# Graph network stack on one Trainium2 core: merge of layer one with both branches normed together, x and rows stored in one step

## The chip, the core and the metric

The kernel runs on one core of one Trainium2 chip. The metric is the time on the device in microseconds (us), from the start to the end of one execution; lower is better. Engines: PE (TensorE), DVE (VectorE), ACT (ScalarE), POOL (GpSimd), SP (SyncE, which here only issues transfers).

## What is computed

A stack of four graph layers over 6250 nodes with 256 features and 106250 edges, each a residual on a pre-normed input. Two places matter here: how layer zero's result enters x, and the end of layer one, where an attention branch over the edges (`h_local`) and a branch from a scan over the nodes sorted by degree (`y`) are merged. Cut to that:

```python
h = maximum(layernorm(x), 0); x = x + L0(h, ...)
h = maximum(layernorm(x), 0)                      # rows, h_dram
# layer one, on h (called x inside the layer)
agg = segment_sum(proj[src] * attn, tgt)
h_local = layer_norm(elu(agg + x + gat_b), ln_local_g, ln_local_b)
y = mamba(x[perm], ...)
h_attn = layer_norm(x + y[inv], ln_global_g, ln_global_b)
gate = sigmoid(h_local @ wl.T + h_attn @ wg.T)
h = gate * h_local + (1 - gate) * h_attn
ff = relu(h @ ff1_w.T + ff1_b) @ ff2_w.T + ff2_b
x = x + layer_norm(h + ff, ln2_g, ln2_b)
h = maximum(layernorm(x), 0)                      # input of layer two
```

## The kernel before

The program is a row of stages, most of them closed by a barrier. Nodes are held in T = 49 blocks of 128 rows. Dense work on nodes runs in *lanes* (`in_lanes`, L163): seven of them, each with its own tile slices, its own PSUM bank and its own semaphore. A job is two blocks (25 jobs, the last of one block). A stage is a Python generator; every `yield` ends a turn of its lane. The program is written turn by turn: in each turn every running lane puts one step into the engines' queues, in lane order, and then `beside` puts in what runs alongside. Lane k starts at turn `stagger * k`; a lane that is done starts its next job three turns later. The engines run their queues in order.

`Chain` (L72 on) makes a lane's steps follow one another. `step` waits on the engine for all that the chain has done so far, issues its instructions and counts the last one. `apart` does the same for instructions on several engines, and counts each. `move` issues transfers from the lane's carrier; whatever step comes next waits for their landing. The carrier is SP for lanes 0, 2, 4 and 6, and POOL for lanes 1, 3 and 5. `layer_norm` (L480) is six steps: statistics (L486) and their aggregation (L489) on DVE, epsilon (L490) on DVE, the power -1/2 on POOL (L491), mean times that on DVE (L492), and scaling on ACT (L493); with gain and shift there are two more on DVE (L496, L497). `turn_blocks` (L509) is a PE step of transposes (L513) and an ACT step that copies them out of PSUM (L518). `elu` (L522) is three steps (L524 to L526).

**Closing stage**, `close_and_project` (L2030), stagger 4. Per job: load of sums, residual rows and x (L2034, L502) and two empty turns; four DVE steps; tanh on ACT (L2043); two DVE steps; elu; one addition (L2047); the store of x (L2048) and two empty turns; the norm; the store of the rows h (L2052); a scatter of h by POOL into the sorted order (L2053) and two empty turns; turning, projection (L2061), copy, scores (L2064), and stores (L2070, L2072). 34 turns.

**Merge**, `merge` (L2499), stagger 8. Beside it, `return_rows` puts one indirect gather per turn on POOL (L2485), 49 in all, which bring the scan's rows back in node order; a semaphore counts each ten of them. Weights are loaded by ACT before (L2461 to L2472) and waited for once, at L2526, in job 0. Per job: load of sums and rows (L2512) and two empty turns; the denominators (L2516 to L2519); agg times their reciprocals (L2521); two additions (L2523, L2527); then the local branch (elu, norm, turning), the wait for the returned rows, the scan branch (addition L2533, norm, turning), the gate's eight products into one bank (L2538), tanh (L2541), three DVE steps (L2542 to L2544), four times a first feed-forward product (L2546) and relu (L2548), the load of x into `ha` (L2549), the second product (L2551) with h added by identity (L2554), the bias (L2557), the norm with gain and shift, the addition to x (L2559), its store (L2560), the last norm and its store (L2562). 63 turns.

The order around the change is thus written by the turn counts alone; there is no planner.

Of the kernel before, what the change touches and what calls it, by code (L numbers as in the profile page):

```python
# [21 lines left out]
ALU = mybir.AluOpType  # L22
ACT = mybir.ActivationFunctionType
# [4 lines left out]
P = 128  # L28
N, D, E = 6250, 256, 106250
T = -(-N // P)  # L30
NP = T * P
TAIL = N - (T - 1) * P
LANES = 7
# [151 lines left out]
def graph_stack_kernel(nc, a, out):  # L185
# [4 lines left out]
    with root:  # L190
        def sem(name):
            return root.enter_context(nc.semaphore(name))
# [11 lines left out]
        sb = maker(root, "sb")  # L204
# [68 lines left out]
        eps = sb("eps", [P, 1])  # L273
        power = sb("power", [P, 2])
        chain.apart((pool, lambda: pool.iota(iota[:, :], [[1, P]], base=0, channel_multiplier=0,
# [233 lines left out]
        def turn_blocks(ch, dst4, src3, ps, gain=None, shift=None):  # L509

            for b in range(0, src3.shape[1], 2):
                m = min(2, src3.shape[1] - b)
                yield ch.step(pe, *[lambda k=k, c=c: pe.transpose(ps[:, c, k, :], src3[:, b + k, c * P:(c + 1) * P], ident[:, :])  # L513
                                    for k in range(m) for c in range(2)])
                if gain is None:
                    yield ch.step(act, lambda: act.activation(dst4[:, :, b:b + m, :], ps[:, :, 0:m, :], ACT.Copy))
                else:
                    yield ch.step(act, *[lambda c=c: act.activation(dst4[:, c, b:b + m, :], ps[:, c, 0:m, :], ACT.Identity,  # L518
                                                                    scale=gain[:, c:c + 1], bias=shift[:, c:c + 1])
                                         for c in range(2)])  # L520

        def elu(ch, x, tmp, out):  # L522

            yield ch.step(dve, lambda: dve.tensor_scalar(tmp, x, 0.0, None, ALU.min))  # L524
            yield ch.step(act, lambda: act.activation(tmp, tmp, ACT.Exp))
            yield ch.step(dve, lambda: dve.scalar_tensor_tensor(out, tmp, -1.0, x, ALU.add, ALU.max))  # L526
# [1456 lines left out]
        with ExitStack() as local:  # L1983
# [34 lines left out]
            with ExitStack() as inner:  # L2018
# [11 lines left out]
                def close_and_project(ch, k, b0, m):  # L2030
# [16 lines left out]
                    yield ch.step(dve, lambda: dve.tensor_tensor(x3, x3, part[0], ALU.add))  # L2047
                    yield ch.move(lambda e: e.dma_start(blk(x_dram), x3))  # L2048
                    yield
                    yield  # L2050
                    yield from layer_norm(ch, x3, t3, stat[:, k, :, :], relu=True)
                    yield ch.move(lambda e: e.dma_start(blk(h_dram), t3))  # L2052
                    yield ch.scatter(pool, *[lambda b=b: pool.indirect_dma_start(  # L2053
# [403 lines left out]
        vecs = {}  # L2457
# [18 lines left out]
        with ExitStack() as local:  # L2476
# [17 lines left out]
            xT, yT = (lsb(n, [P, 2, GB, P]) for n in ("hlT", "haT"))  # L2494
            stat = lsb("stat1", [P, LANES, 2, 8])
            bank = lps("bank2", [P, LANES, 512])
            chain.wait(act)

            def merge(ch, k, b0, m):  # L2499
# [6 lines left out]
                fT += [t3.rearrange("p b d -> p (b d)")[:, j * m * P:(j + 1) * m * P] for j in range(2)]  # L2506
                st, tn = stat[:, k, :, :], bank[:, k, :].rearrange("p (c q n) -> p c q n", c=2, q=2)
                o_ps = bank[:, k, :].rearrange("p (b d) -> p b d", d=D)
# [18 lines left out]
                yield ch.step(dve, lambda: dve.tensor_tensor(l3, l3, bv("gat_b"), ALU.add))  # L2527
                yield from elu(ch, l3, t3, l3)
                yield from layer_norm(ch, l3, l3, st)
                yield from turn_blocks(ch, lT, l3, tn, vecs["ln_local_g"], vecs["ln_local_b"])  # L2530

                dve.wait_ge(returned[b0 // PART_OF], 16 * min(PART_OF, T - b0 // PART_OF * PART_OF))
                yield ch.step(dve, lambda: dve.tensor_tensor(a3, h3, y_all[:, b0:b0 + m, :], ALU.add))  # L2533
                yield from layer_norm(ch, a3, a3, st)
                yield from turn_blocks(ch, aT, a3, tn, vecs["ln_global_g"], vecs["ln_global_b"])
                gT = bank[:, k, 0:2 * m * P].rearrange("p (c b n) -> p c b n", c=2, b=m)
# [8 lines left out]
                for j in range(4):  # L2545
                    yield ch.step(pe, *[lambda c=c: pe.matmul(ff, f1[:, c, j * P:(j + 1) * P], lT[:, c, :, :],  # L2546
                                                              start=(c == 0), stop=(c == 1)) for c in range(2)])
                    yield ch.step(act, lambda: act.activation(fT[j], ff, ACT.Relu, bias=fb[:, j:j + 1]))  # L2548
                yield ch.move(lambda e: e.dma_start(a3, blk(x_dram)))  # L2549
                yield ch.step(pe, *[f for b in range(m) for f in  # L2550
# [6 lines left out]
                yield ch.step(dve, lambda: dve.tensor_tensor(l3, o_ps[:, 0:m, :], bv("ff2_b"), ALU.add))  # L2557
                yield from layer_norm(ch, l3, l3, st, gain=vecs["ln2_g"][:, :], shift=vecs["ln2_b"][:, :])
                yield ch.step(dve, lambda: dve.tensor_tensor(a3, a3, l3, ALU.add))  # L2559
                yield ch.move(lambda e: e.dma_start(blk(merged_x[:, :]), a3))  # L2560
                yield from layer_norm(ch, a3, l3, st, relu=True)
                yield ch.move(lambda e: e.dma_start(blk(hidden[0][0:NP, :]), l3))  # L2562

# [45 lines left out]
```

## Time and profile before

| | us |
|---|---|
| median of 3 runs (lowest, highest) | 7790.14 (7788.18, 7800.23) |
| the profiled execution, its own time | 7791.36 |
| its span, first to last instruction | 7789.4 |
| closing stage of layer zero | about 2674 to 3042 |
| merge of layer one | about 4814 to 5346 |

The profiled execution is 1.2 us above the median. Busy time of an engine is the sum of its instructions; what an engine waited for is read from the waits, where each idle stretch is put down to the semaphore that came last. Landing is the time from a transfer's issue to its last byte's count.

### The profile page before, as it was taken

The numbers are of one execution on the slowest core, as the hardware profiler recorded it, in microseconds if no ns is written. First come the engines' busy times: TensorE is split into PE (matmuls) and PEld (weight loads), VectorE is DVE, ScalarE is ACT, GpSimd is POOL, SyncE is SP. The second block draws the span as 40 slices with busy tenths as digits, with TensorE's granted clock in tenths as the row PEclk, the third lists the DMA queues.
The fourth block names the chain that finished last, engine by engine and source line by source line (L and its number), as shares of the span: only waits on it lengthen the run. The fifth ranks groups of instructions, "written<-read, shape, count | busy, mean of one in ns | idle before, by whom it ended". The sixth has DMA issues, their size and how long they took to land. (4 is left out here: it accounts for less than half of the span.)

```text
span 7789.4 us, 93332 instructions
## 1 busy us (share of the span) xinstructions
PE 5313.0 (68%) x20089; PEld 3414.3 (44%) x20089; DVE 5065.8 (65%) x10805; ACT 3288.2 (42%) x11052; POOL 4469.2 (57%) x4306
## 2 busy tenths in 40 slices
PE   4656688888888545657777774775666665656555
PEld 4623344444444333224444442654444443444444
DVE  7677588888888753569999994664555553333333
ACT  1124466666666423778988894441000000000000
POOL 2150166666666253057777773324777775777775
PEclk9978899999999756779999996997888787888887
DMA  5114488888888663379998996223555556555556
GB/s 197 22 63 110 156 274 278 276 285 278 276 279 280 197 207 117 112 250 321 321 321 316 322 308 167 76 68 107 177 178 180 176 181 126 170 170 165 170 171 134
DMA packets 544576, 1554.19 MB, mean 200 GB/s; under 512 B 135295, under 2 KB 245899, under 8 KB 528650
## 3 DMA queue, kind: packets, MB, share of 16 engines
q0 software_dynamic: 234976, 829.97, 36.1%
q1 hardware_dynamic: 280348, 694.68, 25.2%
q10 hardware_dynamic: 28844, 25.07, 1.0%
q8 instruction: 138, 2.26, 0.1%
q14 instruction: 270, 2.21, 0.1%
HBM read 1183.69 MB, written 593.47 MB: 228 GB/s over the span
## 5 line engine op out<-in xcount | busy, mean ns | idle before, releaser
L1263 POOL DMA_INDIRECT rows_e<-hidden,unit_src x1856 | 1765.5, 951 | 628.5 <-issue 542.9
L618 POOL DMA_INDIRECT rows_e<-table,unit_src x928 | 1071.3, 1154 | 803.9 <-PE acc_e L823 385.8
L1000 POOL DMA_INDIRECT rows_e<-table,unit_src x928 | 1069.1, 1152 | 373.8 <-issue 269.0
L1291 DVE SCALAR_TENSOR_TENSOR sums_e<-sums_e,unit_keep,acc_e 128x256 f32<-128x256 f32 x928 | 444.1, 479 | 1212.1 <-PE acc_e L1372 1209.6
L1372 PE MATMUL acc_e<-rows_e,same 128*128 128x256 f32 x1856 | 707.1, 543 | 666.5 <-DMA rows_e<-hidden,unit_src 651.1
L812 ACT ACTIVATE rows_e<-rows_e 128x64 f32<-128x64 f32 x4640 | 1119.1, 333 | 1.9
L1084 ACT ACTIVATE rows_e<-rows_e 128x64 f32<-128x64 f32 x3712 | 919.9, 333 | 3.8
L1372 PEld LDWEIGHTS acc_e<-rows_e,same 128*128 128x128 f32 x1856 | 487.7, 278 | 845.9 <-DMA rows_e<-hidden,unit_src 708.5
L1416 ACT ACTIVATE turned_f<-turn_f 128x512 f32<-128x512 f32 x98 | 58.5, 597 | 1882.3 <-PE turn_f L1388 1882.3
L823 PE MATMUL acc_e<-rows_e,unit_w 128*128 128x512 f32 (+1 forms) x1856 | 704.9, 526 | 144.7 <-DVE rows_e L805 101.0
L1372 PE MATMUL acc_e<-rows_e,links 128*128 128x256 f32 x1856 | 514.3, 425 | 324.5 <-DMA rows_e<-hidden,unit_src 324.1
L823 PE MATMUL acc_e<-rows_e,hot_e 128*128 128x512 f32 (+1 forms) x1856 | 640.1, 498 | 26.7 <-ACT rows_e L812 20.1
L1372 PEld LDWEIGHTS acc_e<-rows_e,links 128*128 128x128 f32 x1856 | 366.9, 207 | 466.2 <-DMA rows_e<-hidden,unit_src 417.4
L823 PEld LDWEIGHTS acc_e<-rows_e,unit_w 128*128 128x128 f32 x1856 | 353.7, 200 | 424.4 <-issue 355.0
L805 DVE TENSOR_TENSOR rows_e<-rows_e 128x896 f32<-128x896 f32 x464 | 502.3, 1083 | 30.7 <-ACT rows_e L782 29.8
L823 PEld LDWEIGHTS acc_e<-rows_e,hot_e 128*128 128x128 f32 x1856 | 344.4, 190 | 322.2 <-issue 252.6
L847 DVE SCALAR_TENSOR_TENSOR sums_e<-sums_e,unit_keep,acc_e 128x780 f32<-128x780 f32 x406 | 413.5, 1019 | 96.3 <-PE acc_e L823 87.5
L2275 DVE TENSOR_TENSOR_SCAN hs<-decay,state,inp 128x896 f32<-128x896 f32 x224 | 464.2, 2072 | 11.7 <-ACT decay L2286 9.4
L2297 PE MATMUL y_ps<-prod_t,ident 128*128 128x448 f32 x900 | 435.1, 611 | 0.0
L491 POOL TENSOR_TENSOR stat<-stat,power 128x2 f32<-128x2 f32 (+1 forms) x150 | 124.8, 839 | 379.2 <-DVE stat L490 378.2
L1880 PE MATMUL tab_ps<-wt,hn 128*128 128x512 f32 x588 | 308.0, 659 | 1.9 <-DVE score_at L1858 1.9
L2266 DVE TENSOR_TENSOR inp<-bc,dtx_s 128x896 f32<-128x896 f32 x224 | 242.1, 1081 | 4.8 <-issue 4.8
(467 smaller groups left out, 9548.2 us busy)
## 6 DMA issues: line engine op xcount, KB each, us to landing
bc<-bc_rows SPq DMA_DIRECT2D x228, 896.0 KB, 6.6
summed<-sums_e SPq DMA_DIRECT2D x464, 390.0 KB
staged<-sums_e SPq DMA_DIRECT2D x116, 1024.0 KB, 4.5
summed<-sums_e SPq DMA_DIRECT2D x464, 130.5 KB
rows_e<-table,unit_src POOLq DMA_INDIRECT x1856, 5.6
hots<-hot_e SPq DMA_DIRECT2D x116, 256.0 KB, 5.0
hots<-unit_w SPq DMA_DIRECT2D x116, 256.0 KB, 4.9
rows_e<-hidden,unit_src POOLq DMA_INDIRECT x1856, 2.8
```

Source lines behind the costliest of these rows:

```text
L618: pool.indirect_dma_start(self.rows[:, v, e, :], None, table, bass.IndirectOffsetOnAxis(unit_src[:, u, e:e + 1], 0)).then_inc(self.landed[ ...
L805: dve.tensor_tensor(r, r, by.unsqueeze(3).broadcast_to([P, 2, n, DH]), ALU.mult).then_inc(self.s_mul, 1)
L812: last = act.activation(r, r, ACT.Copy, scale=self.rows[:, v, e, self.WIDTH + h:self.WIDTH + h + 1])
L823: mm = pe.matmul(self.acc[:, v % 2, a0:a1], self.hot_of(v)[:, e, :], self.rows[:, v, e, a0:a1], start=(e == 0), stop=(e == 1))
L847: dve.scalar_tensor_tensor(self.sums[:, at_, :], before, unit_keep[:, ds(u, 1)], self.acc[:, v % 2, 0:AW], ALU.mult, ALU.add).then_inc(sel ...
L1000: pool.indirect_dma_start(self.rows[:, v, e, :], None, self.tab, bass.IndirectOffsetOnAxis(unit_src[:, u, e:e + 1], 0)).then_inc(self.land ...
L1084: last = act.activation(r, r, ACT.Copy, scale=self.rows[:, v, e, D + h:D + h + 1])
L1263: pool.indirect_dma_start(self.rows[:, v, e, :], None, tab, bass.IndirectOffsetOnAxis(unit_src[:, u, e:e + 1], 0)).then_inc(self.landed[v ...
L1291: dve.scalar_tensor_tensor(self.sums[:, at_, :], self.sums[:, (n - 1) % self.SUMS, :], unit_keep[:, u:u + 1], self.acc[:, n % self.ACCS, 0 ...
L1372: mm = pe.matmul(self.acc[:, n % self.ACCS, 0:D], self.hot_of(n)[:, e, :], self.rows[:, v, e, :], start=(e == 0), stop=(e == 1))
L2275: dve.tensor_tensor_scan(hs[:, b, :], decay, inp[:, b, :], state[:, ds(STEPS * m + k, 1)], ALU.mult, ALU.add).then_inc(s_scan, 1)
L2297: mm = pe.matmul(y_ps[:, z, 0:HS], ident[:, :], prod[:, b, z * HS:(z + 1) * HS], start=False, stop=False, skip_group_check=True)
```

## The change

`power`, the tile of exponents, becomes four columns wide, and the statistics tile of the merge holds four blocks a lane. In the closing stage the store of x and the store of h become one step behind the norm, and the two empty turns go. In the merge the exponential of elu stands beside the addition of the scan branch; both branches, four blocks, are normed together; the wait for the returned rows comes ahead of the exponential; the scaling of the scan branch runs beside the turning of the local one. The load of x is issued by ACT, on a semaphore of its lane's own, and only the addition waits for it. The two stores at the end become one step.

```diff
-        power = sb("power", [P, 2])
+        power = sb("power", [P, 4])
...
                     yield ch.step(dve, lambda: dve.tensor_tensor(x3, x3, part[0], ALU.add))
-                    yield ch.move(lambda e: e.dma_start(blk(x_dram), x3))
-                    yield
-                    yield
                     yield from layer_norm(ch, x3, t3, stat[:, k, :, :], relu=True)
-                    yield ch.move(lambda e: e.dma_start(blk(h_dram), t3))
+                    yield ch.move(lambda e: e.dma_start(blk(x_dram), x3), lambda e: e.dma_start(blk(h_dram), t3))
...
-            stat = lsb("stat1", [P, LANES, 2, 8])
+            stat = lsb("stat1", [P, LANES, 4, 8])
...
+            x_in, drawn_x = [sem(f"x_in{k}") for k in range(LANES)], [0] * LANES
...
                 yield ch.step(dve, lambda: dve.tensor_tensor(l3, l3, bv("gat_b"), ALU.add))
-                yield from elu(ch, l3, t3, l3)
-                yield from layer_norm(ch, l3, l3, st)
-                yield from turn_blocks(ch, lT, l3, tn, vecs["ln_local_g"], vecs["ln_local_b"])
-
+                yield ch.step(dve, lambda: dve.tensor_scalar(t3, l3, 0.0, None, ALU.min))
                 dve.wait_ge(returned[b0 // PART_OF], 16 * min(PART_OF, T - b0 // PART_OF * PART_OF))
-                yield ch.step(dve, lambda: dve.tensor_tensor(a3, h3, y_all[:, b0:b0 + m, :], ALU.add))
-                yield from layer_norm(ch, a3, a3, st)
-                yield from turn_blocks(ch, aT, a3, tn, vecs["ln_global_g"], vecs["ln_global_b"])
+                yield ch.apart((act, lambda: act.activation(t3, t3, ACT.Exp)),
+                               (dve, lambda: dve.tensor_tensor(a3, h3, y_all[:, b0:b0 + m, :], ALU.add)))
+                yield ch.step(dve, lambda: dve.scalar_tensor_tensor(l3, t3, -1.0, l3, ALU.add, ALU.max))
+
+                both = stat[:, k, 0:2 * m, :]
+                blocks = [(j * m + b, v[:, b, :]) for j, v in enumerate((l3, a3)) for b in range(m)]
+                mean, var = both[:, :, 6], both[:, :, 7]
...
+                yield ch.apart(*[(dve, lambda n=n, v=v: dve.bn_stats(both[:, n, 0:6], v)) for n, v in blocks])
+                yield ch.step(dve, lambda: dve.sem_inc(dve_passed, 1),
+                              *[lambda n=n: dve.bn_aggr(both[:, n, 6:8], both[:, n, 0:6]) for n, _ in blocks])
+                yield ch.step(dve, lambda: dve.tensor_scalar(var, var, 1e-5, None, ALU.add))
+                yield ch.step(pool, lambda: pool.tensor_tensor(var, var, power[:, 0:2 * m], ALU.pow))
+                yield ch.step(dve, lambda: dve.scalar_tensor_tensor(mean, mean, -1.0, var, ALU.mult, ALU.mult))
+                yield ch.step(act, *[lambda n=n, v=v: scaled(n, v) for n, v in blocks[0:m]])
+                yield ch.apart(*turned_to(l3), *[(act, lambda n=n, v=v: scaled(n, v)) for n, v in blocks[m:2 * m]])
+                yield ch.step(act, *copied(lT, vecs["ln_local_g"], vecs["ln_local_b"]))
+                yield ch.step(pe, *[f for _, f in turned_to(a3)])
+                yield ch.step(act, *copied(aT, vecs["ln_global_g"], vecs["ln_global_b"]))
...
-                yield ch.move(lambda e: e.dma_start(a3, blk(x_dram)))
+                ch.wait(act)
+                act.dma_start(a3, blk(x_dram)).then_inc(x_in[k], 16)
+                drawn_x[k] += 16
...
+                dve.wait_ge(x_in[k], drawn_x[k])
                 yield ch.step(dve, lambda: dve.tensor_tensor(a3, a3, l3, ALU.add))
-                yield ch.move(lambda e: e.dma_start(blk(merged_x[:, :]), a3))
                 yield from layer_norm(ch, a3, l3, st, relu=True)
-                yield ch.move(lambda e: e.dma_start(blk(hidden[0][0:NP, :]), l3))
+                yield ch.move(lambda e: e.dma_start(blk(merged_x[:, :]), a3), lambda e: e.dma_start(blk(hidden[0][0:NP, :]), l3))
```

`scaled` is ACT's scaling of one block by its own mean and power, `turned_to` the transposes of one branch, and `copied` the two copies out of PSUM with gain and shift.

## Rows read from the trace of the kernel before

**Rows 1.** The page: busy time, share of the span and instructions of each engine.

```profile
PE 5313.0 (68%) x20089; PEld 3414.3 (44%) x20089; DVE 5065.8 (65%) x10805; ACT 3288.2 (42%) x11052; POOL 4469.2 (57%) x4306
```

**Rows 2.** The windows of the merge: us, busy (x instructions), granted clock, DMA, GB/s.

```profile
4880.00:5312.00 432.00, 333.12 (x1466) 264.94 (x1465) 261.06 (x882) 197.84 (x421) 118.64 (x142) 0.92 0.22 68
4814.00:4880.00 66.00, 18.77 (x63) 14.78 (x64) 25.47 (x87) 15.36 (x33) 48.74 (x51) 0.56 0.53 159
```

**Rows 3.** The waits of 4880 to 5312 us: engine, line, releaser: us, times, longest.

```profile
DVE hl L2557 <- PE bank L2554: 114.6, 23, 8.2
...
PE bank L2546 <- DVE hlT L2544: 39.2, 23, 4.4
...
PE bank L2551 <- DMA ha<-x_dram: 34.7, 19, 3.4
...
PE bank L2546 <- ACT tg L2548: 13.0, 23, 0.6
PE bank L2538 <- ACT haT L518: 9.6, 21, 1.6
DVE stat L486 <- DMA merged_x<-ha: 9.3, 12, 1.2
...
PE bank L2546 <- ACT haT L2548: 2.3, 4, 0.6
```

**Rows 4.** Line 2485: ns min/median/max, first and last start us; landings.

```profile
L2485 POOL DMA_INDIRECT y_all<-sorted_y,rank_i x49: 942/957/1433, 4814.6 to 4895.9; - x49
...
DMA to landing us min/median/max: 2.7/3.0/6.9
```

**Rows 5.** Line 2541, the gate's tanh, same columns.

```profile
L2541 ACT ACTIVATE ha<-bank x25: 383/597/598, 4866.9 to 5311.7; 128x512 f32<-128x512 f32 x24, 128x256 f32<-128x256 f32 x1
```

**Rows 6.** The merge by line and form: count, busy us, mean ns, idle before.

```profile
L491 POOL TENSOR_TENSOR stat<-stat,power 128x2 f32<-128x2 f32 x96 | 83.4, 879 | 202.7 <-DVE stat L490 202.2
...
L492 DVE SCALAR_TENSOR_TENSOR stat<-stat 128x2 f32<-128x2 f32 x96 | 15.4, 161 | 16.4 <-POOL stat L491 15.9
...
L491 POOL TENSOR_TENSOR stat<-stat,power 128x1 f32<-128x1 f32 x3 | 2.1, 706 | 15.0 <-DVE stat L490 15.0
```

**Rows 7.** Transfers: issue, count, size, median us from issue to landing.

```profile
ha<-x_dram SPq DMA_DIRECT2D x14, 256.0 KB, 2.7
merged_x<-ha SPq DMA_DIRECT2D x14, 256.0 KB, 2.1
```

**Rows 8.** Issues on ACT, lines 1435 and 2472: ns min/median/max, starts.

```profile
L1435 ACTq DMA_DIRECT2D hidden<-kept_f x49: 338/343/392, 5455.6 to 6579.8; - x49
...
L2472 ACTq DMA_DIRECT2D unit_w<-w_kept x1: 4022/4022/4022, 4824.9 to 4824.9; - x1
```

**Rows 9.** Line 2549, the load of x, same columns.

```profile
L2549 SPq DMA_DIRECT2D ha<-x_dram x14: 359/360/366, 4882.8 to 5314.8; - x14
L2549 POOL DMA_DIRECT2D ha<-x_dram x11: 590/742/803, 4899.2 to 5328.6; - x11
```

**Rows 10.** The timeline of 4813 to 4842 us: start, us, engine, line, idle before.

```profile
4827.42 0.99 POOL L2485 DMA_INDIRECT y_all<-sorted_y,rank_i  x1 [0.30 <-issue]
...
4836.77 0.69 DVE L2527 TENSOR_TENSOR hl<-hl,v_gat_b 128x512 f32<-128x512 f32 x1 [5.16 <-DMA unit_w<-w_kept]
```

**Rows 11.** The tile of statistics in the merge: ns min/median/max, starts.

```profile
L491 POOL TENSOR_TENSOR stat<-stat,power x99: 557/797/1347, 4840.8 to 5340.3; 128x2 f32<-128x2 f32 x96, 128x1 f32<-128x1 f32 x3
```

**Rows 12.** Line 2043, the tanh of the closing stage, same columns.

```profile
L2043 ACT ACTIVATE rg<-rg x25: 417/630/632, 2685.9 to 2996.0; 128x512 f32<-128x512 f32 x24, 128x256 f32<-128x256 f32 x1
```

**Rows 13.** The waits of 2690 to 3042 us, columns as in rows 3.

```profile
POOL sorted_h L2053 <- DMA h_dram<-tg: 96.3, 21, 7.8
```

**Rows 14.** Transfers of the closing stage, columns as in rows 7.

```profile
x_dram<-xg SPq DMA_DIRECT2D x14, 256.0 KB, 2.6
h_dram<-tg SPq DMA_DIRECT2D x14, 256.0 KB, 2.6
```

**Rows 15.** The window of the closing stage's middle, columns as in rows 2.

```profile
2735.00:2996.00 261.00, 118.61 (x396) 86.89 (x396) 137.59 (x332) 63.87 (x113) 148.15 (x155) 0.59 0.61 200
```

More of the change, by code:

```diff
@@ L2506, in merge @@
                 fT += [t3.rearrange("p b d -> p (b d)")[:, j * m * P:(j + 1) * m * P] for j in range(2)]
-                st, tn = stat[:, k, :, :], bank[:, k, :].rearrange("p (c q n) -> p c q n", c=2, q=2)
+                st, tn = stat[:, k, 0:2, :], bank[:, k, :].rearrange("p (c q n) -> p c q n", c=2, q=2)
                 o_ps = bank[:, k, :].rearrange("p (b d) -> p b d", d=D)
@@ new lines, in merge @@
+                mean, var = both[:, :, 6], both[:, :, 7]
+                scaled = lambda n, v: act.activation(v, v, ACT.Identity, scale=both[:, n, 7:8], bias=both[:, n, 6:7])
+                turned_to = lambda v: [(pe, lambda b=b, c=c: pe.transpose(tn[:, c, b, :], v[:, b, c * P:(c + 1) * P], ident[:, :]))
+                                       for b in range(m) for c in range(2)]
+                copied = lambda to, gain, shift: [lambda c=c: act.activation(to[:, c, :, :], tn[:, c, 0:m, :], ACT.Identity,
+                                                                             scale=gain[:, c:c + 1], bias=shift[:, c:c + 1])
+                                                  for c in range(2)]
```

## The prediction

> **What bounds the kernel now.** Read the page first: no engine is busy over 68% of the span [rows 1], because the program is a row of stages with a barrier between most of them. So a change is priced inside its own stage. Two stages are touched: the one that closes layer zero and projects for layer one (2674 to 3042 us), and the merge of layer one (4814 to 5346 us). Both are written by in_lanes: seven lanes, each working on two blocks of nodes, and one step of each lane per **turn**, put into the engines' queues in lane order. A queue runs in order, so one late step holds the steps of all other lanes behind it.
>
> For the merge I read its windows [rows 2]. In the first 66 us POOL is the busy one (48.7 us: 49 row gathers of 0.96 us, one put in per turn, the last at turn 48 [rows 4]). In the 432 us that follow PE is busy 333 us (77%), DVE 261, ACT 198, POOL 119. The waits of that window [rows 3] account for PE's idle 99 us to the microsecond: 39.2 for the DVE products that open the feed-forward, 34.7 for the load of x, 13.0 and 2.3 for the relu steps, 9.6 for the turned blocks (98.8 in all). PE is the engine that paces the stage, and it stops for four causes only.
>
> **The merge, step by step.** Counting yields: before, a job takes 63 turns and a lane starts again after 66. The local and scan parts take 20 steps (elu 3, norm 6, turning 2, addition 1, norm 6, turning 2); together they take 13. The load of x and the separate store of x have no turn of their own any more. After, 54 turns, and a new start after 57. With stagger 8 and 25 jobs the last job begins at turn 222 before and 195 after. The tanh (L2541) is step 32 before and 25 after, so it stands at turns 31 to 253 before (222 turns, 4866.9 to 5311.7 us, 2.00 us a turn [rows 5]) and at 24 to 219 after. Behind turn 48 there are 205 turns before and 171 after.
>
> *Instructions.* Per job one pow, one addition of epsilon and one mean product fall away, and the pow is of four columns. Pow is 706 ns for one column and 879 for two [rows 6]; 173 ns a column gives an estimate of 1.23 us for four, against 2 x 0.88, so POOL saves 0.5 us a job, and DVE 2 x 0.16 (the mean product's row; the addition is its like). That is 13 and 8 us over the stage on engines that do not pace it: I count nothing. PE's and ACT's arithmetic is the same.
>
> *The load of x.* On the lane's own semaphore the PE step behind it no longer waits: the landing (2.7 us, median [rows 7]) lies beside ten turns. This gives PE the 34.7 us. ACT now issues it: a like issue on ACT takes 0.34 us [rows 8], so 25 x 0.34 = 8.5 us in a queue that is busy 46% of the window; nothing while that cover holds, 8.5 if it is gone. Queued behind ACT's wait are the relus and scalings of other lanes; what ACT waits for is its own relu just before (0.47 us, ending anyway). POOL and SP lose this issue, 11 x 0.74 and 14 x 0.36 us [rows 9]. DVE's new wait for x stands ten turns behind the issue, some 20 us, and passes.
>
> *The two stores in one step.* The norm behind the x store no longer waits for its landing (9.3 us of DVE idle [rows 3]; DVE does not pace, and I count nothing). What is late next is only the lane's own next load, three idle turns later.
>
> *The wait for returned rows* comes ten steps earlier. For job 0 it is at turn 11. Its tenth gather is issued at 4827.4 and the slowest landing was 6.9 us, so 4834.3; DVE stands until 4836.8 for the weights anyway [rows 4, 10]. Nothing. Job 5, the first to use the second part, starts at turn 40, long behind its gathers.
>
> *The sum of the merge.* **Head:** gathers fix the first 48 turns; two pows of 0.88 us fewer there, 2 us. **Middle:** 34 turns fewer. PE's ledger says: 34.7 us of stall go for certain, and of the other 64 us I take the share of the turns that fall away (34 of 432/2.03 = 213, 16%), 10 us: 45. Turns alone at 2.03 us (415.8 us from the last gather to the last tanh, over 205) would say 69, but would put PE at 333/363 = 92% busy. 45 puts it at 86%, and I take that. Lower end 20: the stall goes and 15 us come back as other waits, as lanes stand closer. **Tail:** 31 turns of one short job become 29 and lose two landings, 2.7 and 2.1 us [rows 7]: 5 us, ends 3 and 7. Merge: 52 us, between 25 and 78.
>
> *A rule beside this.* Pow took from 557 to 1347 ns, median 797 [rows 11], so something besides its own work stretches it. The Trainium skill (SBUF — State Buffer, on the shared port pair) says that a VectorE operation with two SBUF inputs and a GpSimd operation that reads SBUF exclude each other for a whole instruction. Denser DVE work would then lengthen pows; this is a rival below.
>
> **The closing stage.** 34 turns a job become 31 and the restart 37 becomes 34: x is stored with h, in one step. With stagger 4, tanh L2043 spans turns 7 to 130 before (310.1 us, 2.52 us a turn [rows 12]) and 7 to 121 after, nine fewer, and the last job's tail is three shorter. But 96.3 us of the stage are POOL standing in 21 waits for h to land, before its scatter [rows 13]. Those come once a job and stay, since the scatter is still the step after the store (and the h store stands 14 turns ahead of its own lane's next loads before, 37 - 23, and after, 34 - 20; with a stagger of 4 that is the same place against the other lanes' loads). Per turn without them: (310.1 - 96.3)/123 = 1.74 us, so 12 turns give 21 us. Against it: the scatter now waits for x as well, which before had two empty turns to land in. The other store's issue is 0.36 (SP) to 0.77 us (POOL), and landings are alike, 2.6 us each from SP [rows 14]; 0.5 us x 21 = 10 us. If the second 256 KB cost their full time at the stage's 200 GB/s [rows 15], 1.3 us x 21 = 27. Net 10 us, between -6 and 28 (12 turns at 2.52 less nothing comes to 30, near that end).
>
> The Trainium skill (DMA: Bandwidth & Descriptors, issuing engines are not separate DMA queues) says transfers issued from any engine interleave on the same 16 engines. By it the pair pays the bytes in full, and the closing stage's result is the lower end.
>
> **Sum:** 52 + 10 = 62 us. The profiled execution took 7791.36 us (span 7789.4 and 2 around it), 1.2 above the median of the three runs, 7790.14; from the median, **7728 us**. About 0.2% (16 us) is what a measurement here can tell from no change.
>
> **Rivals.**
> - *Turns are what is paid* (the grid's latency, not PE's work). For: a turn costs 2.03 us while the pacing engine works 1.56 us in it (333 us over 213 turns). Against: PE would be 92% busy where it is 77%. 2 + 69 + 7 + 28 = 106 us: 7684. Chance 0.22.
> - *Queues are what is paid.* More steps per turn make heads of queues later, DVE idle for the second feed-forward product (114.6 us [rows 3]) above all; the middle gives 15 to 20, the closing stage nothing: 25 us, 7765. Chance 0.14.
> - *No net effect*: as that, and each of the 75 pows costs its longest row, 1.35 - 0.88 = 0.47 us, 35 us in all, which eats the 34.7. Only head and tail are left, 7 us: 7783. It is where the shared-port rule would lead if it held for every pow. For: the spread of the pows. Against: POOL is busy 119 of 432 us, and no wait of PE in [rows 3] is for it. Chance 0.07.
> - *Slower: ACT's issue.* ACT took 4.02 us to issue the load of kept weights [rows 8]; if the 25 loads of x cost 4.02 - 0.34 = 3.7 us more each in front of relus that PE waits for, 92 us come on top: 7790 - 62 + 92 = 7820. It decides from 62/25 = 2.5 us an issue. Against: thirteen other loads of ACT stood in front of that one (L2461 to L2470), and 49 stores in a later stage took 0.34. Chance 0.05.
> - The forecast, 0.52.
>
> **Numbers.** The range runs from the first rival, with room below it, to the second: 7680 to 7765, leaving out the last two and little else. The forecast's own is 7705 to 7750. Faster: 0.52 + 0.22 + 0.14 = 0.88; within 0.2%: 0.07; slower: 0.05.
>
> **What the profile after would show.** PE's wait for x gone; the last tanh some 451 us behind the stage's first instruction instead of 498; PE over 83% busy in the middle; 75 pows in the merge; the scatter's wait for x or h above 96 us; stages outside the two unchanged. Wrong would be: PE's idle as large as before with another name, an x issue on ACT over 1 us, or the closing stage longer by over 10 us.

## The result and the profile after

The changed kernel takes 7668.16 us (median of 4 runs, 7664.3 to 7673.61) against 7789.16 us before in the same session: a ratio of 0.9843 (95% interval 0.9826 to 0.986), 121 us or 1.6% faster. The forecast was faster, by 62 us, with a range down to 7680; the time lies 12 us below it.

Where the time went is read from the barriers between stages (the semaphore waits of SP at L244), in the one profiled execution of each kernel:

| us | before | after | |
|---|---|---|---|
| closing stage (last edge product to barrier) | 393.9 | 379.5 | -14 |
| merge (barrier to barrier) | 542.4 | 429.6 | **-113** |
| of it: to the last row gather (turn 48) | 82.1 | 85.8 | +4 |
| last gather to last tanh | 415.8 | 308.7 | -107 |
| last tanh to the barrier | 44.5 | 35.1 | -9 |
| stage behind the merge, to the end | 2433.2 | 2433.6 | 0 |

The two stages make 127 us; stages that no edit touches differ by 11 us up and down between two profiles, and nearly cancel. First the page's line, then the windows of the merge after; they answer to [rows 1, 2].

```profile
PE 5301.7 (69%) x20089; PEld 3402.6 (44%) x20089; DVE 5059.9 (66%) x10755; ACT 3288.3 (43%) x11052; POOL 4403.2 (57%) x4270
```

```profile
4799.30:4865.00 65.70, 24.36 (x105) 18.70 (x105) 28.94 (x86) 18.64 (x40) 45.55 (x46) 0.69 0.55 167
4865.00:5190.00 325.00, 289.81 (x1399) 232.34 (x1399) 248.98 (x830) 194.31 (x408) 100.20 (x112) 1.00 0.28 87
```

In the middle PE is busy 89% (290 of 325 us) where it was 77%. Its 1399 matmuls take 207 ns each, where 1466 took 227 before (333.12/1466), and the granted clock is 1.00 where it was 0.92. The waits of the middle after (engine, line, releaser: us, times, longest) answer to [rows 3]:

```profile
POOL stat L2545 <- DVE stat L2544: 161.4, 21, 11.9
...
DVE hl L2575 <- PE bank L2572: 42.0, 22, 3.6
...
PE bank L2569 <- ACT tg L2564: 18.9, 22, 2.2
PE bank L2562 <- ACT tg L2564: 12.4, 22, 0.6
...
DVE stat L492 <- POOL stat L491: 5.3, 7, 1.7
```

PE's wait for x is gone, and so is its wait for the DVE products (39.2 before); DVE's idle time in front of the bias, 114.6 before, is 42.0. Of PE's 35 us of idle time in this stretch 31 are two waits for relus, every job the same. The lines of the tanh, of the gathers, and of the load of x on ACT (ns min/median/max, first and last start us) answer to [rows 4, 5, 8]:

```profile
L2557 ACT ACTIVATE ha<-bank x25: 383/597/598, 4843.1 to 5193.8; 128x512 f32<-128x512 f32 x24, 128x256 f32<-128x256 f32 x1
```

```profile
L2482 POOL DMA_INDIRECT y_all<-sorted_y,rank_i x49: 942/953/1521, 4800.1 to 4885.1; - x49
```

```profile
L2566 ACTq DMA_DIRECT2D ha<-x_dram x25: 339/366/372, 4858.1 to 5206.9; - x25
...
DMA to landing us min/median/max: 2.0/2.8/5.0
```

From the last gather to the last tanh are 171 turns in 308.7 us, 1.81 us a turn, against 2.03 before. The issue on ACT takes 0.37 us (0.34 forecast). One job after is like the next; the first window is one job of the kernel after, the three below it are jobs of the kernel before (from tanh to tanh; us, then busy time and count of PE, PEld, DVE, ACT, POOL, then granted clock, DMA share, GB/s):

```profile
4973.90:4988.60 14.70, 13.27 (x66) 10.61 (x65) 11.71 (x39) 9.01 (x19) 4.06 (x6) 1.00 0.40 126
```

```profile
5014.50:5030.20 15.70, 13.13 (x65) 10.58 (x64) 9.16 (x33) 7.93 (x17) 3.83 (x6) 1.00 0.33 102
...
5081.00:5098.90 17.90, 14.47 (x62) 11.38 (x61) 10.12 (x33) 7.19 (x16) 4.38 (x6) 0.90 0.34 104
5098.90:5134.10 35.20, 24.49 (x100) 18.93 (x98) 22.36 (x79) 14.74 (x31) 9.72 (x12) 0.85 0.24 75
```

A job's 66 matmuls cost PE 13.3 us at the full clock; in the second row before, 62 of them cost 14.5, part at the lower level. The last row is the gap between two rounds of starts before, 18 turns, with PE busy 70%. After, the gap has nine turns, and all three gaps take 14.7 us, no more than a regular spacing. How the lower level looks is seen in PE's timeline before (start, us, line, tile, count; four products a row): right after the wait for x they take 1.70 and 1.91 us, the like four later 1.03. The two windows below it give the granted clock: 0.58 behind the wait, 1.00 four microseconds later, so most of the first stretch runs at the lower of the clock's two levels, 1.2 GHz, and the second at the upper, 2.4 GHz.

```profile
5087.26 1.70 PE L2551 MATMUL bank<-f,haT 128*128 128x256 f32 x4 [0.95 <-DMA ha<-x_dram]
5088.75 1.91 PE L2551 MATMUL bank<-f,tg 128*128 128x256 f32 x4
...
5092.08 1.03 PE L2551 MATMUL bank<-f,tg 128*128 128x256 f32 x4
```

```profile
5087.20:5090.40 3.20, 3.14 (x8) 2.55 (x9) 0.46 (x1) 1.76 (x4) 0.00 (x0) 0.58 0.10 32
5091.20:5094.00 2.80, 2.80 (x19) 2.59 (x18) 0.41 (x1) 0.00 (x0) 0.00 (x0) 1.00 0.54 144
```

### The profile page after: what moved, and what is told of

It is laid out like the page before. It is cut to its first block and busy times, and to the rows that moved or that the text cites. A ratio compares the mean times of both kernels' runs of the same rounds, so it can differ in the third digit from the quotient of the medians.

```text
span 7662.5 us, 93224 instructions
## 1 busy us (share of the span) xinstructions
PE 5301.7 (69%) x20089; PEld 3402.6 (44%) x20089; DVE 5059.9 (66%) x10755; ACT 3288.3 (43%) x11052; POOL 4403.2 (57%) x4270
## 5 line engine op out<-in xcount | busy, mean ns | idle before, releaser
L618 POOL DMA_INDIRECT rows_e<-table,unit_src x928 | 1034.1, 1114 | 848.0 <-PE acc_e L823 446.0
L1000 POOL DMA_INDIRECT rows_e<-table,unit_src x928 | 1059.6, 1142 | 375.4 <-issue 270.5
L2279 DVE TENSOR_TENSOR prod_t<-bc,hs 128x896 f32<-128x896 f32 x224 | 241.8, 1080 | 0.0
```

The source lines that it names most:

```text
L618: pool.indirect_dma_start(self.rows[:, v, e, :], None, table, bass.IndirectOffsetOnAxis(unit_src[:, u, e:e + 1], 0)).then_inc(self.landed[ ...
L1000: pool.indirect_dma_start(self.rows[:, v, e, :], None, self.tab, bass.IndirectOffsetOnAxis(unit_src[:, u, e:e + 1], 0)).then_inc(self.land ...
```

## The experiments

All are read by the length of the merge from barrier to barrier in one profile each. It repeats: three kernels with the changed merge gave 429.6, 430.4 and 431.6 us (one of them on a chip whose last stage took 2775 us instead of 2434), two with the merge of before 542.4 and 546.7. Steps of 5 to 7 us in the table are thus hardly more than the 4 us between two profiles of the same merge. No profile of the kernel before was taken on the chip of e9 to e12; that the changed merge takes 430.4 us there says that the merge can be compared across the two. The closing stage took 393.7 to 397.3 us in the ten profiles that have it as before, and 380 to 385 in the five that have it as changed, 13 us less on average. Ratios are to the kernel before on the same chip, with 95% intervals; on the chip of e9 to e12 it took 8322.76 us.

| run | merge, us | ratio |
|---|---|---|
| before | 542.4 | |
| e1 closing stage alone | 546.7 | 0.9983 (0.9973 to 0.9993) |
| e8 x on its own semaphore, turn kept | 498.7 | 0.9938 (0.9916 to 0.996) |
| e2 the same without the turn | 493.2 | 0.9934 (0.9916 to 0.9952) |
| e10 both stores at the end, turn kept | 540.4 | 1.0027 (1.0017 to 1.0037) |
| e4 the same without the turn | 516.2 | 0.9978 (0.9968 to 0.9989) |
| e11 normed together, 7 turns kept | 543.5 | 1.0022 (1.001 to 1.0034) |
| e3 the same without the turns | 509.1 | 0.9968 (0.9953 to 0.9982) |
| e15 x and stores, no turns | 486.4 | 0.994 (0.9921 to 0.996) |
| e6 before, stagger 9 | 571.4 | 1.0038 (1.0025 to 1.0051) |
| e9 as e8, stagger 9 | 467.3 | 0.994 (0.9922 to 0.9958) |
| after | 429.6 | 0.9843 (0.9826 to 0.986) |
| e5 after, nine empty turns a job | 469.5 | 0.9897 (0.9876 to 0.9919) |
| e7 after, stagger 7 | 453.3 | 0.987 (0.9849 to 0.9891) |
| e14 after, x on the chain | 482.6 | 0.9927 (0.9904 to 0.9951) |
| e12 after, closing stagger 5 | 430.4 | 0.9879 (0.9862 to 0.9896) |
| e13 after, x stored last | 431.6 | 0.9875 (0.9854 to 0.9895) |

**e1, the closing stage alone.**

```diff
-                    yield ch.move(lambda e: e.dma_start(blk(x_dram), x3))
-                    yield
-                    yield
                     yield from layer_norm(ch, x3, t3, stat[:, k, :, :], relu=True)
-                    yield ch.move(lambda e: e.dma_start(blk(h_dram), t3))
+                    yield ch.move(lambda e: e.dma_start(blk(x_dram), x3), lambda e: e.dma_start(blk(h_dram), t3))
```

> The kernel before with the closing stage's part of the change alone (x stored together with h, the two empty turns gone). The prediction's sum: 10 us faster than before, between 6 slower and 28 faster. The profile of the changed kernel, stage by stage, says about 17 us faster in this stage. If the second store costs its full bytes in front of the scatter, 0 to 6 us slower. Merge as before, 536 us between its barriers.

Measured: 13 us faster by the ratio, and the stage is 380.4 us long against 393.9 (the 536 us of the expectation count the merge up to SP's arrival at the barrier, 542 up to its leaving). The waits of the stage in this run show that POOL stands for h less than before, 82.4 us against 96.3 [rows 13]:

```profile
POOL sorted_h L2050 <- DMA h_dram<-tg: 82.4, 20, 7.1
```

**e2, x on its own semaphore without a turn, and e8, with an empty turn in its place.**

```diff
-                yield ch.move(lambda e: e.dma_start(a3, blk(x_dram)))
+                ch.wait(act)
+                act.dma_start(a3, blk(x_dram)).then_inc(x_in[k], 16)
+                drawn_x[k] += 16
+                yield            # e8 alone
...
+                dve.wait_ge(x_in[k], drawn_x[k])
                 yield ch.step(dve, lambda: dve.tensor_tensor(a3, a3, l3, ALU.add))
```

> The kernel before with only the load of x issued by ACT on its own semaphore and without a turn of its own (period 65 turns instead of 66). Ledger theory (PE's idle time for x is simply given back): 35 to 42 us faster, PE's wait for x gone. Spacing theory (what matters is that job starts come evenly, and the gap between two rounds of starts is still 17 turns against 18): 10 to 25 us faster, since PE stands elsewhere instead; granted clock in the merge's middle stays near 0.92. Turn theory (2.0 us a turn): 3 turns, 6 us.

> The kernel before with the load of x on its own semaphore from ACT, but with an empty turn kept in its place, so that the turn grid (66 turns, same order of everything else) is that of before. Ledger theory: 35 us faster. If the stall is only pushed on to the next cause (the products behind DVE's chain): 5 to 15 us faster. Its difference to the run without the empty turn is what the turn itself is worth: 6 us by the turn theory.

Measured: the wait is worth 43.7 us with the grid untouched, more than the 35 of the ledger; the turn another 5.5, near the spread of two profiles. Spacing was expected to eat half of it, and does not. The window of e8's middle, and its waits, show that DVE's products hold PE as before:

```profile
4876.30:5276.00 399.70, 326.38 (x1492) 263.77 (x1491) 264.15 (x895) 201.43 (x428) 114.18 (x136) 0.92 0.23 73
```

```profile
PE bank L2547 <- DVE hlT L2545: 39.4, 23, 4.1
```

Where the surplus comes from, the whole stage shows better than its middle. These are the second product's rows from 4814 to 5350 us before, and from 4809 to 5310 us in e8 (count, busy us, mean ns, then PE's idle time in front):

```profile
L2551 PE MATMUL bank<-f,haT 128*128 128x256 f32 x196 | 63.5, 454 | 43.3 <-DMA ha<-x_dram 43.3
L2551 PE MATMUL bank<-f,tg 128*128 128x256 f32 x196 | 60.8, 441 | 0.0
```

```profile
L2555 PE MATMUL bank<-f,haT 128*128 128x256 f32 x196 | 55.2, 408 | 2.2 <-ACT tg L2549 2.2
L2555 PE MATMUL bank<-f,tg 128*128 128x256 f32 x196 | 50.8, 382 | 0.0
```

PE stood 43.3 us for x in the whole stage, not 34.7: rows 3 count only 4880 to 5312 us. And the products behind the load ran partly at the lower clock; without the stall these two rows cost 18 us less. All 1584 matmuls of the stage cost 365.4 us before and 350.4 in e8. The 58 us of both are not kept whole: about 15 come back as other idle time of PE.

**e3, the branches normed together, and e11, with seven empty turns ahead of the gate.** The edit is the norm part of the change, as in its diff; e11 adds

```diff
+                for _ in range(7):
+                    yield
                 gT = bank[:, k, 0:2 * m * P].rearrange("p (c b n) -> p c b n", c=2, b=m)
```

> The kernel before with only the two branches made first and normed together (13 steps for 20, period 59 turns, gap of 11 turns between rounds of starts). Ledger theory: the wait for x stays, 10 to 25 us faster. Spacing theory: 60 to 85 us faster, the second product's starts 15 to 16.5 us apart also from round to round, granted clock 0.96 or more. Turn theory: 28 turns of 2.0 us, 56 us.

> The kernel before with both branches normed together and seven empty turns kept ahead of the gate, so that the gate and all behind it stand on the turns of before and only the contents of the first part are changed. Without the empty turns the merge was 509 us, 33 shorter than before. Turn theory: the empty turns take all of that back, 535 to 545 us. If one pow less per job and the shorter chain are what counts: 510 to 520 us.

Measured: 33 us with seven turns fewer, which no theory's range held, and nothing with the turns kept (543.5 against 542.4). One pow less a job, 25 in all, is worth nothing here; the turns are all of it. It is less than the 56 us of the turn theory. The three gaps between rounds gave back 40 us (105.1 to 65.0), but the spacings inside the rounds grew by 19 (339.7 to 358.4), and PE's wait for x stays and is longer than before: 40.3 us in the middle, against 32.1 in the like stretch before.

```profile
PE bank L2569 <- DMA ha<-x_dram: 40.3, 20, 4.5
```

**e4, both end stores in one step, and e10, with an empty turn where the first stood.**

```diff
                 yield ch.step(dve, lambda: dve.tensor_tensor(a3, a3, l3, ALU.add))
-                yield ch.move(lambda e: e.dma_start(blk(merged_x[:, :]), a3))
+                yield            # e10 alone
                 yield from layer_norm(ch, a3, l3, st, relu=True)
-                yield ch.move(lambda e: e.dma_start(blk(hidden[0][0:NP, :]), l3))
+                yield ch.move(lambda e: e.dma_start(blk(merged_x[:, :]), a3), lambda e: e.dma_start(blk(hidden[0][0:NP, :]), l3))
```

> The kernel before with only the two stores at the end of a merge job in one step (period 65 turns, gap 17). Ledger theory: 0 to 4 us faster (one landing of the tail, PE waits for none of it). Turn theory: 3 turns, 6 us. Spacing theory: 2 to 8 us faster. A saving over 12 us would say that DVE's 9 us of waiting for the store was on the path and is amplified.

> The kernel before with both stores of a merge job issued at its end but an empty turn kept where the store of x stood, so that only DVE's wait for that store's landing is gone and the grid is that of before. Storing in one step without the turn made the merge 26 us shorter. If the wait for the landing was what cost: merge 516 to 525 us. Alignment theory (the missing turn moved the load of x behind more PE work, whose wait fell from 32 to 11 us): this run gives 534 to 542 us, with PE's wait for x at 28 us or more.

Measured: 26 us without the turn, over three times what any theory gave, and 2 us with it kept. DVE's wait for the landing costs nothing. The middle's waits tell what the missing turn did: PE's wait for x is 10.6 us in e4 and 34.2 in e10.

```profile
PE bank L2551 <- DMA ha<-x_dram: 10.6, 11, 1.8
```

```profile
PE bank L2551 <- DMA ha<-x_dram: 34.2, 17, 3.2
```

A lane restarts one turn sooner, so other lanes' matmuls stand in front of the load of x differently. That they cover more of it is how I read the shorter wait; no run shows it apart.

**e15, both of these without their turns.** e2 and e4 together.

> The kernel before with the load of x on its own semaphore without a turn, and both end stores in one step (period 64 turns). Storing in one step alone gave 26 us, taken for the shift of x behind more PE work, since without the missing turn it gave 2. With x out of the way that should be gone and only the turn is left: merge 483 to 490 us (493 with x alone). If the parts simply add: 467 us.

Measured: 486.4 us, 6.8 below e2. With x out of the way the stores' 26 us are gone and a turn's worth is left: the parts of the change do not add where two of them shorten the same wait.

**e6, the kernel before with stagger 9, and e9, the same on e8.**

```diff
-            in_lanes(lanes, merge, 8, return_rows(), 1)
+            in_lanes(lanes, merge, 9, return_rows(), 1)
```

> The kernel before with a stagger of 9 in place of 8 in the merge: no step changed, job starts 9 turns apart and a gap of 12 turns between rounds (was 18), three turns more in all. Spacing theory: 20 to 45 us faster than before, granted clock above 0.95. Turn theory: three turns more, 6 us slower. Ledger theory: no change, within 6 us.

> The kernel before with the load of x on its own semaphore and an empty turn kept for it (as in the run before of that kind, merge 499 us between its barriers, 66 turns), and a stagger of 9 in place of 8. In the kernel before, a stagger of 9 made the merge 29 us longer, with PE's wait for x grown from 32 to 83 us. Alignment theory (what a shift of the grid changes is which PE work stands in front of the load of x): without that wait stagger 9 costs nothing or gains, merge 475 to 505 us. If the shift itself is bad (three turns more, other queues clash): 515 to 530 us.

Measured: 29 us slower in e6, which felled the spacing theory as I had put it; PE's wait for x had grown to 83.4 us.

```profile
PE bank L2551 <- DMA ha<-x_dram: 83.4, 19, 5.9
```

With that wait taken away first, the same stagger is 31 us faster (467.3 against 498.7, on two chips), past the end of what was expected, at a clock of 0.96 against 0.92:

```profile
5048.00:5429.00 381.00, 318.38 (x1501) 256.00 (x1501) 271.07 (x924) 198.35 (x435) 125.15 (x148) 0.96 0.26 79
```

So spacing counts after all, once no transfer stands in the path. These two edits, with nothing of the norm, give 75 us of the merge's 113.

**e5, the changed kernel with nine empty turns at the end of a job, and e7, with stagger 7.**

```diff
+                for _ in range(9):
+                    yield
```

```diff
-            in_lanes(lanes, merge, 8, return_rows(), 1)
+            in_lanes(lanes, merge, 7, return_rows(), 1)
```

> The changed kernel with nine empty turns at the end of each merge job, so that a lane starts again after 66 turns, as before, with the changed kernel's steps (gap of 18 turns between rounds of starts). Spacing theory: 45 to 60 us slower than the changed kernel, with a gap of some 33 us between the last start of a round and the first of the next and a granted clock of 0.9 to 0.95. Ledger theory (PE's work and its stalls for single causes set the time, empty turns cost nothing where PE has work): under 15 us slower. Against the kernel before: 65 to 80 us faster by the spacing theory.

> The changed kernel with a stagger of 7 in place of 8 in the merge: no step changed, gap of 15 turns between rounds of starts (was 9), three turns fewer in all. Spacing theory: 15 to 40 us slower than the changed kernel. Turn theory: 6 us faster. Ledger theory: within 6 us of it.

Measured: 40 us slower in e5, for 27 more turns up to the last start, 1.5 us each, just short of the 45 to 60 of the spacing theory; 24 us slower in e7, though it has three turns fewer, as that theory had it. In both the jobs inside a round still start 14 to 15 us apart, and the gap between rounds takes 30 us (18 turns) and 27 (15 turns) instead of 15. A matmul in e5's middle takes 215 ns at a clock of 0.97:

```profile
4856.00:5168.80 312.80, 265.93 (x1235) 211.09 (x1234) 216.14 (x713) 169.45 (x355) 92.99 (x106) 0.97 0.28 84
```

So in the changed kernel a job inside a round takes 14.7 us (13.3 of PE's work, 1.4 for relus), and with seven turns between starts instead of eight hardly less, 14.4 in e7's full rounds; what is left to lose is the gap.

**e14, the changed kernel with the load of x back on the chain.**

```diff
-                ch.wait(act)
-                act.dma_start(a3, blk(x_dram)).then_inc(x_in[k], 16)
-                drawn_x[k] += 16
+                yield ch.move(lambda e: e.dma_start(a3, blk(x_dram)))
...
-                dve.wait_ge(x_in[k], drawn_x[k])
```

> The changed kernel with the load of x back on the lane's chain, as a step with a turn of its own (period 58 turns). In the kernel before, taking this wait away without the turn gave 44 us and with it 49. If the parts simply add: merge 430 + 49 = 479 us. If alignment decides: PE's wait for x depends on which PE work stands in front of it in that turn, and may be anything from 10 to 85 us; merge 440 to 500 us, and the growth over 430 is about that wait plus half-clock stretches.

Measured: 53 us slower (482.6); the semaphore is worth here about what it is worth in the kernel before, 49. PE's wait for x was 25.2 us in the 350 us from 4850 on:

```profile
PE bank L2566 <- DMA ha<-x_dram: 25.2, 18, 4.5
```

**e12, stagger 5 in the closing stage, and e13, x stored in the last step.**

```diff
-                in_lanes(lanes, close_and_project, 4)
+                in_lanes(lanes, close_and_project, 5)
```

```diff
-                    yield ch.move(lambda e: e.dma_start(blk(x_dram), x3), lambda e: e.dma_start(blk(h_dram), t3))
+                    yield ch.move(lambda e: e.dma_start(blk(h_dram), t3))
...
-                    yield ch.move(lambda e: e.dma_start(blk(table1), o3), lambda e: e.dma_start(blk(dst1), sc1[:, b0:b0 + m, :]))
+                    yield ch.move(lambda e: e.dma_start(blk(table1), o3), lambda e: e.dma_start(blk(dst1), sc1[:, b0:b0 + m, :]),
+                                  lambda e: e.dma_start(blk(x_dram), x3))
```

> The changed kernel with a stagger of 5 in place of 4 in the closing stage (a lane restarts after 34 turns, so that job starts come 5 turns apart, 4 between rounds, where they were 4 and 10). In the merge even spacing kept PE at work once no transfer stood in its way. Here POOL stands for the landing of h (83 us of waits). If evenly spaced loads clash less with these stores: closing stage 355 to 372 us (380 in the changed kernel), 8 to 25 us faster in all. If turns set it: 6 more turns for the last start, less the shorter gap already counted, 5 to 12 us slower.

> The changed kernel with the closing stage's store of x moved once more, from the store of h to the last step of the job, so that POOL's scatter waits for h alone; no turn is added. My sum charged the pair of stores 10 us (0.5 us in each of 21 waits), up to 27. If the pair costs that: closing stage 360 to 372 us (380 in the changed kernel) and POOL's waits for h 8 to 25 us less. If the second store's landing costs nothing because the waits are for the loads of other lanes in front of h: 377 to 383 us.

Measured: the closing stage is 387.9 us in e12 and 390.7 in e13, 8 and 11 longer than in the changed kernel's profile, but only 2.5 and 5 above the longest of the five like stages (385.4, in e14); e12 ran on the slower chip, and that it is slower at all is not shown. The 8 to 25 us that even spacing was to give did not come: POOL's waits for h are 76.3 us there against 82.7, and the stage is no shorter. In e13 POOL's waits are 79.9 us against 82.7 after, so the second store cost the scatter next to nothing, and moving it away wins nothing. What makes the stage longer with the store at the end of the job stays open. The waits of the stage in e13 and after:

```profile
POOL sorted_h L2050 <- DMA h_dram<-tg: 79.9, 15, 7.1
```

```profile
POOL sorted_h L2050 <- DMA h_dram<-tg: 82.7, 19, 7.1
```

No version beat the changed kernel. The ratios of e9 to e15 stand 9 to 25 us less favourable than their stages (e10: 2 us shorter merge, ratio 1.0027). Stages that no edit touches took 1434 to 1475 us (edges of layer one) among profiles on like chips; which of them moves in these, and why, was not tried, and verdicts here rest on the stages. By the ratios alone e10 and e11 would be 22 and 18 us slower than before.

## Why the forecast was too small

**Right:** that the time lies in the two stages alone; that PE paces the merge, and that its wait for x goes in full; the turn counts (the runs with turns kept and left out go by them), and the three pows a job; ACT's issue at 0.37 us for 0.34, with nobody waiting; POOL's four-column pow (1.32 us on average, 1.23 estimated), a bystander, worth nothing (e11); the store of x that DVE waited for, nothing (e10); the returned rows, nothing seen. The closing stage: 10 us forecast, 14 measured and 13 on average over the profiles, by another sum than mine. I gave 21 us to turns and took 10 off for the pair of stores; e13 shows that the scatter does not pay for the pair.

**The step that failed:** "PE's ledger says: 34.7 us of stall go for certain, and of the other 64 us I take the share of the turns that fall away ... 10 us: 45. Turns alone at 2.03 us ... would say 69, but would put PE at 333/363 = 92% busy." I set the two counts against each other and took the smaller. They are different things, and in this change both came. One term was too small besides: the stall stood at 34.7 us, from the middle alone, and is 43.3 in the whole stage; taking it away gave 43.7 (e8). The runs build the merge up one by one:

| | merge, us | gives |
|---|---|---|
| before | 542.4 | |
| wait for x gone, all turns kept (e8) | 498.7 | 43.7 |
| its turn (e2) | 493.2 | 5.5 |
| the stores' turn (e15) | 486.4 | 6.8 |
| normed together, seven turns (after) | 429.6 | 56.8 |

The three last make 69 us for 36 turns fewer in the whole stage (285 to 249), 1.9 us each on average: near the turn rival's price. On top of it stands the wait, 44 us. In my split: the middle gave 107 us, which is 34 turns at 2.03 (69) and 171 turns at 1.81 instead of 2.03 (38). Head and tail, 2 and 5 forecast, gave -4 and 9.

A turn has no fixed price, though: e9 has three turns more than e8 and is 31 us shorter, e7 three fewer than the changed kernel and is 24 us longer. The starts of the 25 tanh tell why. Of their 24 spacings 21 lie inside a round of seven starts and three are the gaps between rounds (us, with the turns of each in brackets):

| | barrier to first tanh | 21 spacings in rounds | 3 gaps | last tanh to barrier |
|---|---|---|---|---|
| before | 53.1 | 339.7 (8) | 105.1 (18) | 44.5 |
| e8 | 55.1 | 307.2 (8) | 99.1 (18) | 37.2 |
| e15 | 54.5 | 305.4 (8) | 91.7 (16) | 34.8 |
| after | 43.8 | 306.6 (8) | 44.1 (9) | 35.1 |
| e7 | 43.8 | 294.6 (7) | 81.5 (15) | 33.3 |
| e9 | 51.6 | 322.7 (9) | 58.3 (12) | 34.7 |

The stall of PE lay mostly inside the rounds: with it gone they take 307 us instead of 340 and stay there. The 27 turns that the change takes out between the first and the last start all lie in the three gaps, and are worth 2.0 us each there (99.1 to 44.1). At nine turns a gap is as short as any other spacing. e9 gains by shorter gaps more than it loses in its rounds; e7 does the reverse.

Why the cap on PE was wrong is in the windows. Two figures were taken as fixed. *PE's work, 333 us*, had half-clock stretches in it: 1466 matmuls at after's 207 ns are 304 us, 29 less. *PE's other idle time*, 64 us, was to shrink with the turns, by 16%; scaled to the same matmuls it is 37 us (35.2 x 1466/1399), 27 less instead of 10. The 39.2 us for DVE's products went entirely, and DVE's own idle time ahead of the bias fell from 114.6 to 42.0. So 92% busy was no bar: with the work at 304 us, the 363 us that the turns alone gave would have had PE busy 84% of the time.

**The rivals.** Turns as the price (7684, chance 0.22) was nearest, 16 us too high, for it left out what PE's stall gives by itself. Queues as the price and no net effect are refuted for this grid: with more steps in each turn the turn got cheaper. The shared port of VectorE and GpSimd (the Trainium skill, SBUF — State Buffer, SBUF: two separate sides) made no difference that a run could show: pow's median was 797 ns before [rows 11], and the two-column ones after took 692, with DVE busy 77% of the middle instead of 60%. The slower rival, ACT's issue, did not come: its longest took 0.37 us.

```profile
L491 POOL TENSOR_TENSOR stat<-stat,power x50: 551/692/1181, 4871.7 to 5217.8; 128x2 f32<-128x2 f32 x48, 128x1 f32<-128x1 f32 x2
```

The Trainium skill (DMA: Bandwidth & Descriptors, issuing engines are not separate DMA queues) pointed to the lower end for the closing stage, since a pair of stores shares the 16 engines. The measurement decides against the size that I gave it, not the rule: that POOL's waits fell from 96.3 to 82.7 us beside twice the bytes, together with e13's 79.9 for h alone, says that these waits are hardly for the stores' own bytes.

## What to carry to other kernels

In a pipeline written turn by turn, price a change twice and add the two: the stall that it takes off the pacing engine, whole stage and not only its middle, and the turns that it takes out of the gap between two rounds of starts. Most of what the turns gave lay there (55 of 69 us; 11 more came ahead of the first tanh); inside a round the pacing engine set the spacing once the transfer was off the path (e8, e15, after). Do not cap the gain by the pacing engine's busy time before you have looked at its granted clock, because the stalls that go may have cost it the clock. And a transfer waited for in the path makes every other edit of the grid unreadable (one turn less gave 26 us, one more of stagger cost 29): take it off the path first, then tune the spacing so that the restart comes about lanes times stagger turns apart.

## What the runs showed that was not expected

The granted clock in the merge's middle was higher in the runs in which PE was busy for more of it: 0.92 before, with PE busy 77% (matmuls 227 ns), 0.92 in e8 at 82% (219 ns), 0.96 in e9 at 84% (212 ns), 1.00 after at 89% (207 ns). The drop shows in stretches of a few products right behind PE's waits (1.91 us for four, then 1.03). By the mean of a matmul it was worth 29 of the 91 us that the middle gained for the same number of them; over the whole stage the same 1584 matmuls cost 365.4 us before and 330.7 after. Which idle stretch brings the clock down stays open: a job before with the same three waits (0.56, 1.47 and 0.98 us) kept 1.00.
